# The bias seeded into the accumulator by ScalarE, with the attention steps regrouped in each slot

## The reference

```
# attention: a low-rank adapter picked by sample, then autocorrelation
y    = A[id] @ (B[id] @ x)                      # rank 16
f    = rfft(y);  corr = irfft(f * conj(f))
w, d = top_k(corr, 6);  w = softmax(w)          # int(log(1024)) = 6 delays
x    = x + sum_k w[k] * roll(y, d[k])
# feed-forward: mix the channels, then a routed low-rank expert layer
z    = weights[cond]^T @ x                      # 64 x 64 by sample
p    = softmax(z @ W_router^T); top 2, made to sum to 1
out  = x + z @ W_base^T + b_base + 2 * sum_e p[e] * (z @ A_e^T) @ B_e^T
```

## Time and profile before

| | |
|---|---|
| median of the runs | 849.53 us (3 runs, 848.49 to 856.43) |
| the profiled execution | 851.39 us, span 849.6 us from the first to the last instruction |
| granted TensorE clock, mean | 0.969 of 2.4 GHz |
| PE busy | 788.3 us, 93% of the span |
| DVE busy | 655.4 us, 77% |
| POOL busy | 510.5 us, 60% |
| ACT busy | 328.2 us, 39% |

### The profile page before, as it was taken

The page is one execution under the profiler, slowest core; times in us unless marked ns, Lnnn a source line. Parts: engine busy times, 40 slices in busy tenths (PEclk is TensorE's granted clock), DMA queues, the critical chain, the costliest instruction groups (busy, mean ns, idle before and its releaser), DMA issues.

```text
span 849.6 us, 14441 instructions
## 1 busy us (share of the span) xinstructions
PE 788.3 (93%) x4828; PEld 657.8 (77%) x4828; DVE 655.4 (77%) x1387; ACT 328.2 (39%) x624; POOL 510.5 (60%) x447
## 2 busy tenths in 40 slices
PE   2967799999999999999999999999999999999897
PEld 2755678788878888788888888788878887877786
DVE  1256688988878787988878787988888788888952
ACT  3455344333543444333543444333533442333211
POOL 0123476757678766757677766757677664566621
PEclk9866799999999999999999999999999999999999
DMA  7769577887877888888877888887877877875521
GB/s 208 221 181 246 197 243 255 261 221 222 267 252 220 242 260 252 262 221 237 252 240 243 234 261 247 263 225 220 271 233 248 239 230 227 262 237 191 189 84 50
DMA packets 65661, 193.48 MB, mean 228 GB/s; under 512 B 13548, under 2 KB 23180, under 8 KB 62484
## 3 DMA queue, kind: packets, MB, share of 16 engines
q0 software_dynamic: 23040, 83.90, 33.9%
q1 hardware_dynamic: 31988, 72.93, 30.2%
q10 hardware_dynamic: 10560, 35.75, 10.8%
HBM read 117.82 MB, written 50.33 MB: 198 GB/s over the span
## 4 chain that ended last, share of the span: by engine, by line
PE 55%; POOL 15%; DVE 13%; issue 7%; DMA 5%; ACT 4%; SPq 1%; ACTq 1%; POOLq 0%; DVEq 0%
PE o_ps L502 27%; PE h_ps L640 5%; PE x_ps L526 5%; DMA y_d<-y 4%; PE c_ps L502 4%; POOL rolled L1266 3%; POOL turn L1289 3%; POOL eo L1293 3%; POOL row L1250 3%; PE t_ps L575 2%; PE t_ps L598 2%; PE x_ps L508 2%; ACT eo_hi L888 2%; PE x_ps L629 2%; POOL eo L1292 2%
## 5 line engine op out<-in xcount | busy, mean ns | idle before, releaser
L1266 POOL DMA_INDIRECT rolled<-y_d,off x160 | 203.9, 1274 | 218.2 <-DVE row L1073 105.2
L1073 DVE SCALAR_TENSOR_TENSOR row<-rolled,weight,row 128x1024 f32<-128x1024 f32 x160 | 222.1, 1388 | 10.2 <-DMA rolled<-y_d,off 3.9
L502 PE MATMUL o_ps<-wt_hi,x_hi 128*128 128x512 f32 x512 | 219.3, 428 | 0.0
L502 PE MATMUL o_ps<-wt_hi,x_lo 128*128 128x512 f32 x512 | 203.2, 397 | 0.0
L502 PE MATMUL o_ps<-wt_lo,x_hi 128*128 128x512 f32 x512 | 202.9, 396 | 0.0
L502 PEld LDWEIGHTS o_ps<-wt_hi,x_hi 128*128 128x128 f32 x512 | 97.4, 190 | 22.2 <-issue 4.6
L502 PEld LDWEIGHTS o_ps<-wt_hi,x_lo 128*128 128x128 f32 x512 | 96.4, 188 | 23.4
L502 PEld LDWEIGHTS o_ps<-wt_lo,x_hi 128*128 128x128 f32 x512 | 96.9, 189 | 15.7
L1250 POOL TENSOR_TENSOR row<-row,bias 128x1024 f32<-128x1024 f32 x32 | 77.7, 2427 | 16.3 <-PE x_ps L629 15.8
L849 ACT ACTIVATE turn<-t_ps 128x512 f32<-128x512 f32 x64 | 35.0, 596 | 101.5 <-PE t_ps L575 101.5
L1289 POOL TENSOR_TENSOR turn<-turn 128x256 f32<-128x256 f32 x64 | 71.7, 1141 | 2.6
(11 more groups left out here) (156 smaller groups left out, 1505.6 us busy)
## 6 DMA issues: line engine op xcount, KB each, us to landing
y_d<-y ACTq DMA_DIRECT2D x64, 512.0 KB, 3.6
row<-in_x SPq DMA_DIRECT2D x32, 512.0 KB, 7.7
out<-row SPq DMA_DIRECT2D x32, 512.0 KB, 6.1
adapter<-g_hi SPq DMA_DIRECT2D x62, 256.0 KB, 6.5
adapter<-g_lo SPq DMA_DIRECT2D x31, 256.0 KB, 6.7
r<-in_L_cond_A SPq DMA_DIRECT2D x60, 64.0 KB, 3.5
r<-in_L_cond_B SPq DMA_DIRECT2D x56, 64.0 KB, 5.9
rolled<-y_d,off POOLq DMA_INDIRECT x160, 7.1
```

The costliest lines, as they stand in the source:

```text
L502: last = pe.matmul(dst, a, b, start=start and n == 0, stop=stop and n == len(todo) - 1)
L1073: dve.scalar_tensor_tensor(rows[:, :], from_buffer[:, :], weight[:, n:n + 1], rows[:, :], ALU.mult, ALU.add).then_inc(sum_step, 1)
L1266: pool.indirect_dma_start(out=rolled[at % RB][:, :], out_offset=None, in_=y2_d[u], in_offset=bass.IndirectOffsetOnAxis(ap=off[s % 2][:, n: ...
```

## The change

Four things are done at once.

- ACT copies the bias into `o_ps` after each output add (`bias_seeded`, counted by the new semaphore `seeded`), behind its `mixed_out`. The PE's `base` waits for `seeded` in place of `out_add`, and only tile 0 still begins its sums afresh. POOL's `bias_added` is left for tile 0 alone, and stands behind that slot's gathers.
- On the PE, `x_transposed` moves from behind chunk 0 to behind `project`, and `b_times_x`, `bx_repeated`, `spectrum` and `adapter_out` each move up by one chunk.
- On DVE, `bx_masked` moves between rolls 3 and 4, and `weights` and `add_y` move behind router half 1.
- On ACT, `x_out` stands ahead of `fold_out`, and the pieces of the adapter spectra move: `a_out` behind `square`, `a_high` and `b_out` behind `y_copy`.

The core of the diff:

```
         def base(t, c):
                 if c == 0 and t > 0:
-                    pe.wait_ge(out_add, t)
+                    pe.wait_ge(seeded, t)
...
-                     (wt_hi[:, c, cols], wt_lo[:, c, cols]))], c == 0, False)
+                     (wt_hi[:, c, cols], wt_lo[:, c, cols]))], c == 0 and t == 0, False, True)
...
                 if ffn:
                     project(t)
+                if attn:
+                    x_transposed(s, 0)
+                    x_transposed(s, 1)
                 for c in range(KC):
                     if ffn:
                         base(t, c)
...
-                    if c == 0 and attn:
-                        x_transposed(s, 0)
-                        x_transposed(s, 1)
+                    if c == 1 and attn:
+                        b_times_x(s, u, i)
                     if c == 2 and attn:
-                        b_times_x(s, u, i)
+                        bx_repeated(s)
...
                     if c == 3 and attn:
-                        bx_repeated(s)
+                        spectrum(s, u, i)
...
                     if c == 4 and attn:
-                        spectrum(s, u, i)
+                        adapter_out(s, u)
...
-                    if c == 5 and attn:
-                        adapter_out(s, u)
...
+            def bias_seeded(t):
+
+                act.wait_ge(out_add, t)
+                act.activation(o_ps[:, :], bias[:, :], ACT.Copy).then_inc(seeded, 1)
...
                 if has(m):
                     mixed_out(m)
+                if has(t) and has(m):
+                    bias_seeded(m)
...
                 if has(m):
                     add_rolled(m, 3)
-                    add_rolled(m, 4)
                 if attn:
                     bx_masked(s)
-                if has(last):
-                    weights(last)
-                    add_y(last)
+                if has(m):
+                    add_rolled(m, 4)
                 if attn:
                     stack_low(s)
                 if has(t):
                     router(t, 1)
+                if has(last):
+                    weights(last)
+                    add_y(last)
...
-                    dve.wait_ge(biased, t + 1)
+                    if t == 0:
+                        dve.wait_ge(biased, 1)
...
-                if has(t):
-                    bias_added(t)
                 if has_attn(s):
                     powers(s)
                 if has(last):
                     gather(last, (u - 1) % U, range(3, NSEL))
+                if t == 0:
+                    bias_added(0)
```

More of the change, by code:

```diff
@@ L298, in tiles @@
         biased = sem("biased")
+        seeded = sem("seeded")
         fold_step = sem("fold_step")
@@ L496, in _, with three @@
         def _(pe):
-            def three(dst, pairs, start, stop):
+            def three(dst, pairs, start, stop, seeded_dst=False):
                 n, last = 0, None
@@ L501, in three @@
                 for a, b in todo:
-                    last = pe.matmul(dst, a, b, start=start and n == 0, stop=stop and n == len(todo) - 1)
+                    last = pe.matmul(dst, a, b, start=start and n == 0, stop=stop and n == len(todo) - 1,
+                                     skip_group_check=seeded_dst)
                     n += 1
@@ L661, in experts @@
                     last = three(o_ps[:, cols], [((ht_hi[:, :], ht_lo[:, :]), (bs_hi[:, cols], bs_lo[:, cols]))],
-                                 False, True)
+                                 False, True, True)
                 last.then_inc(out_mm, 1)
@@ L697, in slot @@
                         fold_transposed(g)
-                    if c == 0 and attn:
-                        x_transposed(s, 0)
-                        x_transposed(s, 1)
+                    if c == 1 and attn:
+                        b_times_x(s, u, i)
                     if c == 2 and attn:
-                        b_times_x(s, u, i)
-                    if c == 2 and u == 0 and prep and ffn:
-                        pe.wait_ge(x2_l, 2 * t + 2)
+                        bx_repeated(s)
                     if c == 2 and u == 0 and prep:
+                        if ffn:
+                            pe.wait_ge(x2_l, 2 * t + 2)
                         a_transposed(g)
                     if c == 3 and attn:
-                        bx_repeated(s)
+                        spectrum(s, u, i)
                     if c == 3 and u == 2 and prep:
@@ L901, in slot @@
                 attn, prep = has_attn(s), has_group(g)
+                if attn:
+                    x_out(s, t)
                 if prep and u == 2:
                     fold_out(g)
-                if attn:
-                    x_out(s, t)
                 if has(last):
@@ L911, in slot @@
                                    accum_out=rsum[:, :]).then_inc(rexp_out, 1)
+                if attn:
+                    stack_high(s)
+                    square(s)
                 if prep and u == 0:
@@ L914, in slot @@
                 if attn:
-                    stack_high(s)
+                    y_copy(s)
                 if prep and u == 2:
                     a_high(g, u, i)
-                if attn:
-                    square(s)
-                if prep and u == 2:
                     spectrum_high(g)
@@ L923, in slot @@
                     b_out(g)
-                if attn:
-                    y_copy(s)
                 if has(t):
```

## The result

The changed kernel takes 824.09 us (median of 4 runs, 822.35 to 826.14), the kernel before 852.98 us in the same comparison (4 runs, 848.49 to 856.76): ratio 0.9655, 95% interval 0.9612 to 0.9698. The forecast was 823.5. The profiled execution took 822.35 us with a span of 820.5 us.

A forecast was written before the change was run, and what follows sets the result against it. The PE sets the pace, so only its waits can be won: 16.9 us in six periods, the rest in slots 0 and 25 to 29, less 0.8 for seeds, together 26.0 off 849.53, giving 823.5 us; range 816 to 840.

The forecast's parts named there:

- 2.82 us per period: Gain over four successive slots, one of each kind: 3.42 us of PE waits less 0.4 and 0.2 kept; six periods, 16.9.
- kind 0: Slot type of 23.33 us in the profile before: 1.18 us lost ahead of `correlation`, all to be covered.
- kind 2: Slot type of 26.43 us, PE busy throughout: nothing to win, 0.2 us of new wait from ACT's reordered copies.
- The bias add off POOL: 31 of 32 POOL adds of 2.43 us go: little on the path by itself, but 3.4 us in slot 25.
- slot 25: Slot of 25.07 us, DVE's add of `y` taking 4.05 us beside POOL's bias add: 3.4 us to win.
- The attention a chunk earlier: PE's attention steps come 1.49 us earlier, covering `correlation`'s waits: 1.18 us in kind 0, 0.47 in kind 3, 1.26 in slot 26.
- kind 3: Slot type of 22.54 us in the profile before: 0.47 us lost ahead of `correlation`, to be covered.
- `hc` ahead of `weights`: On DVE, an add of at least 1.29 us leaves `hc`'s way: kind 1's wait goes, slot 29 gains 2.2 us.
- Rival 2: Lock moves from bias add to `powers`, holding add of `y`, roll 0 and roll 1: slower, 860 us; chance 0.04.
- Kinds 1 and 2: Slot types of 23.05 and 26.43 us: to keep 0.4 us of 1.77 lost, and 0.2 us of new wait.
- The seed: ACT's bias copy of 1.03 us: nothing in slots with attention, 0.4 us in each of the last two, -0.8 us.

The follow-up runs named there:

- seed alone: Kernel before, with ACT's bias seed and POOL's bias adds removed but for tile 0's, all orders as before: 832.64 us, ratio 0.971-0.977.
- order alone: Kernel before, with the new orders on PE, DVE and ACT but no seed, POOL adding every bias ahead of `powers`: 866.12 us, ratio 1.010-1.017.
- `bx_masked` undone: Changed kernel with `bx_masked` moved behind roll 4 again: 832.81 us, ratio 0.972-0.981 against the kernel before.

## Why the prediction was right, and where its reasons were wrong

The sum was right because it was made from what the PE waited for, slot by slot, and from the longest wait that could be left. Whatever held DVE and ACT, its price on the path was those waits.

How near it came is partly luck. The 2.82 us per period came true to 0.01 in the one period shown, with errors that cancel: kind 0 gained 1.01 us where 1.18 was forecast, kind 2 0.02 where it was to lose 0.2. The means over slots 2 to 24 give 3.05 per period. The gain was forecast at 26.0 us and is 28.9 by the medians; 823.5 is so near 824.09 because the forecast started from a median of 849.53, where the comparison has 852.98.

Point by point:

- **The bias add off POOL** was the step that failed: "On the path this is worth little by itself", argued from POOL waiting for `square` 21 of 29 times. POOL was indeed in time, within 0.08 us in 28 of 29 slots, but DVE was not: that its short rows were held by the add was put at nothing outside slot 25. The seed alone brings 22 of the 29 us. The same hold as in slot 25 sat in `rp` or its neighbours all over the kernel, and a median of 1.6 us for a row of 128x2 would have told it.
- **The attention a chunk earlier** does cover the correlation waits: from the seed alone to the changed kernel, kind 0 drops by 0.75, kind 1 by 0.5 and kind 3 by 0.22 us, 8.2 us over slots 2 to 24. But only together with `bx_masked` and ACT's moves, which cost 8.7 and 18.5 us if they are left out, and only with the seed: without it the order loses 11 us.
- **`hc` ahead of `weights`** was credited with its wait in kind 1 and with slot 29. It is worth nothing in this kernel: the seed had already taken those waits away.
- **Rival 2**, slower by the lock, was given 0.04 and 860 us. Its mechanism is real, with the bias add for `powers` in its place: the order alone takes 866 us, and `ht_lo` ends 18.46 us into the slot, where the rival had 18.4. That the two agree is chance: the rival held three rows for about 0.9 us each, and the run has one of 2.29 with smaller ones behind it. In the changed kernel the add is gone and no roll beside `powers` lasts over 1.83 us.
- **Kinds 1 and 2** were to keep 0.4 and 0.2 us. Kind 1 keeps 0.28 (21.56 - 21.28), kind 2 nothing; kind 0 keeps 0.2 that was not counted, since `eo_lo` is still a little late there. Gather 1's instruction in slot 14 takes 0.94 us, not 1.93. Roll 4 still runs beside it, but starts 0.24 us behind it (432.45 and 432.21) where it had started 0.16 us ahead (444.21 and 444.37); with `bx_masked` undone roll 4 is ahead again, and the instruction takes 1.93.
- **The seed** costs nothing in a slot with attention and 0.55 us, not 0.4, in each of the last two. Tile 0's late add makes `base` start 0.57 us later in slot 1 (3.21 against 2.64), and slot 1 is 0.55 us longer than before; slot 0 is 1.2 us shorter.

Open stays why with the seed alone `correlation` is hardly late any more in four slots of kind 3 (1.70 to 1.75 us behind `mixed` in slots 12 to 24, before 2.14 to 2.17) and still late in the others, and how the 42 us of the order alone, less the 8 of the clock, divide between DVE's held row and ACT's wait for the add of `y`; both come from the same add.

## What to carry to other kernels

A wait list says what the bound engine waits for, and that sizes a gain; it doesn't say why the work behind it is late. Look at the rows of short operations on the engines in between: here rows that lasted ten times their least were held by a neighbour, though no wait showed it. And edits that are right together can be worse than nothing one by one: test them in the combination that you mean to keep. A forecast can also be right in its sum and wrong in what it credits: only the edits one by one showed that.

## What the hardware showed that I had not expected

- A TENSOR_SCALAR row of DVE of 0.23 us is held for the whole of POOL's add, 2.52 us beside 2.39 and 1.42 beside 1.29, while DVE rows that read PSUM run at their usual 0.69 us beside such an add, and a RECIPROCAL row on SBUF alone at its usual 0.16.
- POOL's gather instruction takes 1.93 us when it starts beside a roll of DVE that already runs, and 0.94 when the roll starts behind it, and in the one pair of slots compared an earlier issue did not bring the data sooner.
- After about 2 us without a matmul in kind 1 of the order alone the PE ran some three and a half microseconds at 1.2 GHz, which cost 1.6 us a slot. The kernel before has one such stretch, in slot 25, behind a wait of 1.98 us (0.93 of the clock over the slot).
